# A four-stage graph attention, FFN and Mamba kernel: channel-major first attention, a masked attention that projects last, and a new order of the steps

## The reference, cut to what matters

```
def gat(inp, mask, W, a):
    h = inp @ W
    e = leaky_relu(h @ a[:F] (column) + h @ a[F:] (row), 0.2)
    e = where(mask > 0, e, -9e15)            # not in the first attention
    return elu(softmax(e, axis=2) @ h)

# layer 0
o1  = relu(ln(x) @ mlp1_w + b)               # 256 -> 512
z1  = elu(gat(o1, None, W_fc, a_fc)) + o1    # first attention, 512 channels, no mask
o2  = relu(z1 @ mlp2_w + b)                  # 512 -> 256
x1  = x + relu(elu(gat(o2, adj, W_hand, a_hand)) + o2)    # masked attention "b"
x2  = x1 + ln(x1) + ffn of the 127 nodes with the largest routing weight, times the weight
# layer 1
x3  = x2 + elu(softmax(masked leaky scores) @ (ln(x2) @ W))    # masked attention "g"
out = x3 + mamba2_block(ln(x3))
```

## Time and profile before

| | us |
|---|---|
| median of 3 runs (lowest, highest) | 3889.12 (3888.59, 3889.54) |
| the profiled execution, its own time | 3887.89 |
| its span, first to last instruction | 3886.2 |
| TensorE matmul busy, share of the span | 3668.9, 94% |
| VectorE, ScalarE, GpSimd busy | 3107.9, 2355.4, 1002.1 |
| one full turn (start of L1378 to its next start, from 2008.89) | 57.18 |

### The profile page before, as it was taken

One profiled execution on the slowest core, in us unless ns is written; L12 is line 12 of the kernel. 1 busy time (PEld: TensorE's weight loads), 2 busy tenths in 40 slices (PEclk: granted clock), 3 DMA queues, 4 the chain that ended last, 5 costly groups with the idle time before them and its releaser, 6 DMA issues.

```text
span 3886.2 us, 64302 instructions
## 1 busy us (share of the span) xinstructions
PE 3668.9 (94%) x21016; PEld 3171.3 (82%) x21016; DVE 3107.9 (80%) x8243; ACT 2355.4 (61%) x5250; POOL 1002.1 (26%) x1817
## 2 busy tenths in 40 slices
PE   3789999999999999999999999999999999999985
PEld 2578888888888888888888888888888888888864
DVE  2358888888888888888888888888888888888875
ACT  1246666666666666666666666666666666666654
POOL 0012223223222222322322222232232222223222
PEclk8889999999999999999999999999999999999987
DMA  3000010010011001001001100100100110010000
GB/s 92 11 23 28 30 38 27 30 38 33 24 38 38 27 30 38 27 30 38 32 25 38 38 27 30 38 27 30 38 31 26 38 38 27 30 38 27 30 28 30
DMA packets 73763, 126.85 MB, mean 33 GB/s; under 512 B 9984, under 2 KB 64128, under 8 KB 65536
## 3 DMA queue, kind: packets, MB, share of 16 engines
q1 hardware_dynamic: 73728, 126.42, 9.6%
HBM read 109.10 MB, written 17.30 MB: 33 GB/s over the span
## 4 chain that ended last, share of the span: by engine, by line
PE 68%; DVE 22%; ACT 5%; issue 4%; DVEq 0%; POOL 0%; DMA 0%; POOLq 0%
PE A L1179 12%; PE M L1315 7%; PE A L1199 6%; PE A L1217 6%; PE Q L1303 6%; PE M L1349 6%; PE A L1264 3%; DVE yss L1109 3%; PE A L1226 3%; PE Q L1226 3%; PE Q L1264 3%; DVE u L875 3%; DVE ga_ L1003 2%; PE A L1209 2%; DVE acc L1050 2%
## 5 line engine op out<-in xcount | busy, mean ns | idle before, releaser
L1179 PE MATMUL A<-w_fc,o1T 128*128 128x256 f32 (+1 forms) x2048 | 460.9, 383 | 3.7 <-ACT o1T L619 3.7
L1179 PEld LDWEIGHTS A<-w_fc,o1T 128*128 128x128 f32 x2048 | 382.5, 189 | 65.0 <-ACT o1T L619 5.3
L535 POOL TENSOR_TENSOR var_m<-mv_m,epsilon 128x2 f32<-128x2 f32 x64 | 12.5, 195 | 1414.5 <-DVE mv_m L818 1414.5
L786 ACT ACTIVATE dec<-cumB,cumcol 128x256 f32<-128x256 f32 (+1 forms) x1024 | 366.3, 443 | 0.0
L1041 DVE SCALAR_TENSOR_TENSOR acc<-M,w_conv,acc 128x255 f32<-128x255 f32 (+2 forms) x768 | 315.0, 470 | 0.0
L1315 PE MATMUL M<-xT_m,w_in 128*128 128x256 f32 x1280 | 297.5, 379 | 0.9 <-DVE tz L1083 0.8
L1199 PE MATMUL A<-h,low 128*128 128x257 f32 (+1 forms) x1024 | 256.6, 395 | 22.5 <-DVE low L859 14.0
L1315 PEld LDWEIGHTS M<-xT_m,w_in 128*128 128x128 f32 x1280 | 237.8, 190 | 32.2 <-DVE tz L1083 2.1
L1296 PE MATMUL Q<-selT,w_up 128*128 128x128 f32 x2048 | 249.5, 275 | 0.9 <-ACT selT L722 0.9
L1217 PE MATMUL A<-e,w_mlp 128*128 128x256 f32 x1024 | 242.8, 391 | 1.5 <-DVE e L883 1.5
L1303 PE MATMUL Q<-w_down,gsq 128*128 128x256 f32 x1024 | 237.0, 385 | 7.1 <-DVE gsq L1014 7.1
(11 more groups left out here) (236 smaller groups left out, 8901.8 us busy)
## 6 DMA issues: line engine op xcount, KB each, us to landing
cumB<-cum_dram SPq DMA_DIRECT2D x64, 1024.0 KB, 4.7
x_in<-in_x SPq DMA_DIRECT2D x64, 256.0 KB, 2.8
x<-in_x SPq DMA_DIRECT2D x64, 256.0 KB, 3.0
out<-x3b SPq DMA_DIRECT2D x64, 256.0 KB, 2.9
w_mlp<-in_L_gnn_mlp_w SPq DMA_DIRECT2D x2, 512.0 KB, 5.6
w_fc<-in_L_gnn_W_fc SPq DMA_DIRECT2D x2, 512.0 KB, 6.3
w_up<-in_L_ffn_w SPq DMA_DIRECT2D x1, 1024.0 KB, 10.1
w_down<-in_L_ffn_w SPq DMA_DIRECT2D x1, 1024.0 KB, 11.3
```

Source lines behind the costliest of these rows:

```text
L786: last = nc.scalar.activation(dec[:, h, :], columns[:, h, :], ACT.Relu, bias=cumcol[:, i, h:h + 1], scale=-1.0)
L1179: last = nc.tensor.matmul(rows1(half, u, 2), o1T[:, k, u * P:(u + 1) * P], w_fc[:, k, half, 0:D + 2 * i], start=(k == 0), stop=(k == KH - 1))
```

## The change

It has five parts.

1. **First attention, channel-major.** Everything between `a_fc` and `a_mlp2` now has channels on the partitions. The row sums are formed before the product: `a_sums` (ScalarE: two exp of the spread row, one of the ends, two scaled copies; VectorE: two multiply-max with accumulate, a reciprocal), `a_spread` (TensorE: two transposes; VectorE: one multiply of the factors), `a_low` (ScalarE: two scaled copies, before part of `a_factors`). `a_att` has h1 stationary and p1 moving, so the eight transposes of `a_uturn` and the column of ones are gone. The elu works in halves of 512 columns. `a_mlp1`, `a_turn` and `a_mlp2` all use bank A1, one after the other.
2. **Second masked attention.** The two score columns come from VectorE (four multiply-accumulates over 256 channels, `g_proj`), P @ xn is formed first (`g_att`, turned) and then projected (`g_proj` on TensorE). The four transposes of `g_turn` are gone; ScalarE copies yT instead of xT_g and no longer writes hp_g.
3. **Routing.** `q_route_col` is gone (ScalarE adds the bias to the column), and the rank is one instruction per tile instead of two.
4. **Mamba.** bT and cT get 128 partitions, the upper 64 zero; `m_sq` is two tensor_tensor additions.
5. **A new order and new lags on every engine.** Head steps have lag 0 where they had 1, b_ steps on TensorE 1 where they had up to 2; VectorE now has lags up to 7, ScalarE up to 6, SP up to 8.

```diff
     "tensor": [
+        ("q_gather", 3), ("g_proj", 4), ("a_att.0", 1), ("a_att.1", 1), ("m_cum_col", 5), ("q_ffn1.0", 3),
+        ("q_ffn1.1", 3), ("a_mlp2", 1), ("a_turn", 0), ("m_cb", 5), ("b_proj", 1), ("a_mlp1.0", 0), ("b_bcast", 1),
+        ("b_res", 1), ("m_xrow", 5), ("q_ffn2", 3), ("a_mlp1.1", 0), ("q_scatter", 3), ("m_y.0", 5), ("b_pturn", 1),
+        ("m_y.1", 5), ("b_att", 1), ("a_fc.0", 0), ("m_out", 5), ("m_turn", 4), ("g_bcast", 3), ("m_ss", 5),
+        ("a_fc.1", 0), ("m_dt", 4), ("m_z", 4), ("a_bcast", 0), ("q_route", 2), ("g_pturn", 3), ("m_xbc_a", 4),
+        ("g_att", 3), ("m_xbc_b", 4), ("a_spread", 0), ("m_da", 4),
     "vector": [
+        ("g_proj", 5), ("m_norm", 6), ("b_elu_c", 3), ("b_x1", 3), ("m_sq", 7), ("a_fc", 2), ("g_mask", 5),
+        ("m_ms", 7), ("q_stats", 3), ("a_stats", 0), ("g_lrelu", 5), ("a_fcol", 2), ("m_dt", 6), ("m_out", 7),
+        ("g_max", 5), ("m_gate", 6), ("a_maxima", 2), ("q_rank", 4), ("a_sums", 2), ("g_pturn", 5), ("a_spread", 2),
+        ("m_scan", 6), ("a_probs", 2), ("m_conv_b.0", 6), ("m_conv_b.1", 6), ("m_conv_b.2", 6), ("m_cum_col", 6),
+        ("g_elu_b", 5), ("a_elu_c", 2), ("q_norm", 3), ("q_gelu_a", 4), ("m_silu", 6), ("q_route", 3),
+        ("q_gelu_b", 4), ("a_norm", 0), ("b_proj", 2), ("m_cb", 6), ("q_ffn2", 4), ("m_mix.0", 6), ("b_mask", 2),
+        ("b_lrelu", 2), ("g_x3", 5), ("m_mix.1", 6), ("q_scatter", 4), ("m_stats", 5), ("b_max", 2), ("q_x2", 4),
+        ("g_stats", 4), ("m_y.0", 6), ("m_y.1", 6), ("g_norm", 4), ("b_pturn", 2),
     "scalar": [
+        ("m_decay.1", 6), ("m_xrow", 6), ("a_mlp1", 1), ("b_exp", 2), ("b_pturn", 2), ("b_att", 2), ("b_elu_b", 2),
+        ("m_gated", 6), ("m_turn", 5), ("m_dt_exp", 5), ("g_exp", 4), ("m_z", 5), ("q_route", 3), ("a_fcol", 1),
+        ("g_pturn", 4), ("a_sums", 1), ("m_xbc_a", 5), ("g_turn", 4), ("a_factors", 1), ("m_xbc_b", 5), ("a_low", 1),
+        ("q_gather", 3), ("g_att", 4), ("g_elu", 4), ("a_att", 1), ("a_elu_b", 1), ("m_silu", 5), ("m_decay.0", 5),
+        ("a_mlp2", 1), ("q_gelu_a", 3), ("a_turn", 0), ("q_gelu_c", 3), ("b_proj", 1),
     "gpsimd": [
+        ("m_da", 6), ("a_norm", 0), ("q_norm", 3), ("m_turn", 6), ("m_xrow", 6), ("m_norm", 5), ("q_turn", 3),
+        ("g_norm", 4), ("m_rms", 6), ("m_dt_log", 5),
     "sync": [
+        ("m_spread", 7), ("a_load", 0), ("m_store", 8), ("a_residual", 3),
...
+            def a_sums(b):                                   # ScalarE
+                act.wait_ge(S["gcol_ready"], b)
+                for i, rate in enumerate((1.0, ALPHA)):
+                    last = nc.scalar.activation(brow[:, i, :], A1[:, N:2 * N], ACT.Exp, bias=falls[:, i:i + 1], scale=rate)
+                last.then_inc(S["brow_ready"], 1)
+                act.wait_ge(S["ends_ready"], nth(b, 2, 2))
+                nc.scalar.activation(ends[:], ends[:], ACT.Exp).then_inc(S["ends_exp"], 1)
...
+                    last = nc.scalar.activation(low[:, u, :], brow[:, 1, :], ACT.Copy, scale=ends[:, 1, u:u + 1])
+                last.then_inc(S["part_ready"], 1)
...
+            def a_elu_c(b):                                  # VectorE
+                for i, ps in enumerate((A0, A2)):
+                    v.wait_ge(S["e1x_ready"], nth(b, 2, i + 1))
+                    half = e1[:, 2 * i:2 * i + 2, :]
+                    nc.vector.tensor_tensor(half, two(ps), half, ALU.max).then_inc(S["u1_ready"], 1)
+                for i in range(2):
+                    v.wait_ge(S["u1_ready"], nth(b, 2, i + 1))
+                    half = e1[:, 2 * i:2 * i + 2, :]
+                    nc.vector.scalar_tensor_tensor(out=half, in0=half, scalar=-1.0, in1=o1T[:, 2 * i:2 * i + 2, :],
+                                                   op0=ALU.add, op1=ALU.add).then_inc(S["z1_ready"], 1)
...
+            def g_proj(b):                                   # VectorE
+                v.wait_ge(S["g_xn"], b)
+                before(v, S["g_ue"], b)
+                for u in range(U):
+                    for end in range(2):
+                        last = nc.vector.scalar_tensor_tensor(out=(ea, sc)[end]["g"][:, u, :], in0=xn["g"][:, u, :], scalar=1.0,
+                                                              in1=w_ends[:, end, :], op0=ALU.mult, op1=ALU.mult,
+                                                              accum_out=fc["g"][:, u, end:end + 1])
...
             def m_sq(b):
-                nc.vector.tensor_reduce(yss[:], ysq.rearrange("p k n -> p n k"), AX_X, ALU.add)\
-                    .then_inc(S["yss_ready"], 1)
+                nc.vector.tensor_tensor(ysq[:, 0:2, :], ysq[:, 0:2, :], ysq[:, 2:4, :], ALU.add).then_inc(S["sq_half"], 1)
+                v.wait_ge(S["sq_half"], b)
+                nc.vector.tensor_tensor(yss[:], ysq[:, 0, :], ysq[:, 1, :], ALU.add).then_inc(S["yss_ready"], 1)
...
             def a_att(b, half):                              # TensorE
+                for c in range(2):
                     for j in range(U):
+                        last = nc.tensor.matmul((A0, A2)[half][:, c * N:(c + 1) * N], h1[:, j, half, c * P:(c + 1) * P],
+                                                p1[:, j, :], start=(j == 0), stop=(j == U - 1))
...
-            def a_uturn(b):
-                pe.wait_ge(S["u1_ready"], b)
...
             def a_mlp2(b):
-                pe.wait_ge(S["z1_ready"], b)
+                pe.wait_ge(S["z1_ready"], nth(b, 2, 2))
...
-                a_turn=turn_rows("a", A0, "b_sc"), g_turn=turn_rows("g", Q0),
+                a_turn=turn_rows("a", A1, "o2_ready"), 
```

More of the change, by code:

```diff
@@ L17 @@
 NEG = 9.0e15
+LEAST = 2.0 ** -126
 GELU_CUBE = 0.044715
@@ L29 @@
     "tensor": [
[L30 to L34, removed]
@@ L449, in _ @@
                     last.then_inc(PEs, 1)
+                pe.wait_ge(DV, DV_ENDS)
+                for half in range(2):
+                    for t in range(KD):
+                        last = nc.tensor.transpose(Q0[:, half * D + t * P:half * D + (t + 1) * P],
+                                                   w_gat[:, t, D + half:D + half + 1].to_broadcast([P, P]), ident[:])
+                last.then_inc(PEs, 1)
                 pe.wait_ge(DV, DV_TURNED)
@@ L796, in _ @@
             turns(nc.scalar, "scalar", dict(
-                a_turn=evac_T("a", A0), g_turn=evac_T("g", Q0), m_turn=evac_T("m", M0),
-                a_mlp1=a_mlp1, a_fcol=a_fcol, a_factors=a_factors, a_att=a_att, a_elu_b=a_elu_b, a_mlp2=a_mlp2,
-                b_proj=proj("b", (A0, A2)), g_proj=proj("g", (Q0, Q1)),
-                b_exp=softmax("b"), g_exp=softmax("g"), b_pturn=pturn("b", A2), g_pturn=pturn("g", Q1),
-                b_att=elu_exp("b", A2), g_att=elu_exp("g", Q1), b_elu_b=b_elu_b, g_elu=g_elu,
+                a_turn=evac_T("a", A1), g_turn=g_turn, m_turn=evac_T("m", M0),
+                a_mlp1=a_mlp1, a_fcol=a_fcol, a_factors=a_factors, a_sums=a_sums, a_low=a_low, a_att=a_att, a_elu_b=a_elu_b, a_mlp2=a_mlp2,
+                b_proj=proj("b", (A0, A2)),
+                b_exp=softmax("b"), g_exp=softmax("g"), b_pturn=pturn("b", A0), g_pturn=pturn("g", Q1),
+                b_att=elu_exp("b", A0, -1.0), g_att=elu_exp("g", Q1, 0.0), b_elu_b=b_elu_b, g_elu=g_elu,
                 q_route=q_route, q_gather=q_gather, q_gelu_a=q_gelu_a, q_gelu_c=q_gelu_c,
@@ L880, in a_uturn @@
[L880 to L886 removed]
+                v.wait_ge(S["r1_ready"], nth(b, 2, 1))
@@ L1173, in a_fc @@
             def a_fc(b, i):
-                pe.wait_ge(S["o1_ready"], b)
+                if i == 0:
+                    pe.wait_ge(S["o1_ready"], nth(b, 2, 2))
+                else:
+                    before(pe, S["v1_ready"], b)
                 half = 1 - i
@@ L1189, in a_bcast, with a_spread @@
                     for u in range(U):
-                        last = spread_column(A2[:, half * N + u * P:half * N + (u + 1) * P], f1[:, u, half:half + 1])
+                        last = spread_column(A1[:, half * N + u * P:half * N + (u + 1) * P], f1[:, u, half:half + 1])
                 last.then_inc(S["fb_ps"], 1)
+            def a_spread(b):
+                pe.wait_ge(S["r1_ready"], nth(b, 2, 2))
+                pe.wait_ge(S["h1_a"], b)
+                for u in range(U):
+                    last = spread_column(A0[:, u * P:(u + 1) * P], r1[:, u:u + 1])
+                last.then_inc(S["rb_ps"], 1)
             def a_att(b, half):
```

260 lines of the change are left out of this document (132 added, 128 removed).

## The result

The changed kernel takes 3996.62 us (median of 4 runs, 3994.83 to 4001.50) against 3888.91 of the kernel before in the same comparison: ratio 1.0279, interval 1.0261 to 1.0297. It is slower, as forecast, but by 108 us instead of 15, and outside the range of 3825 to 3955. The profiled execution took 3998.37 us, its span is 3996.7.

What follows compares the result with a forecast made beforehand. TensorE was taken as the bound, but waits would bring the turn to 57.7 us (54.25 work + 3.1 waits + 0.35 restarts) against 57.18: 3887.9 + 30 - 15 gives 3903, or 3904 beside the median; range 3825 to 3955.

Steps and rivals of the forecast that it cites:

- everything asked for is there in time: From a_turn through a_mlp1, b_, m_y and a_fc to the end of m_z, no step would wait for its input.
- I price it at nothing: GpSimd's m_turn waits for the store but ends an estimated 2 us before m_xrow has its input; cost nothing.
- other steps as the closest: Between a_turn and m_z, least time to spare: b_pturn 0.2 to 0.3 us, m_xbc_a 0.4, m_ss 1.3.
- The chain from the end of `m_z`: Through ScalarE, VectorE and a_mlp2 to a_turn, 24.3 us, against 21.2 us of TensorE work; TensorE waits 3.1 a turn.
- what is taken off TensorE comes back as waiting: Full turn: TensorE's work falls 1.27 us to 54.25, but waits make the turn 57.7 us against 57.18.
- rivals 1 and 2: 1: TensorE bound, waits unchanged, 3792 us, chance 0.15 (halfway 3855, 0.17). 2: no change, 3880 to 3896, chance 0.18.
- Rival 3: ScalarE's m_decay.0, 1.1 us to spare, ends late ahead of a_mlp2; 0.9 us a turn, 3960 us, chance 0.12.
- the sum: Whole time: 58 turns at 0.5 us give +30, the drain -15, fill even; 3903, or 3904 beside the median.
- the fill: The fill and 1 us more of setup, taken as even, with 15 us either way.
- the drain: Last five intervals, 245.0 us before: emptier turns earlier give -15 us, bounds nothing and about 10 a turn for two turns.
- the gain of 0.18: m_cb on TensorE: 128 instead of 64 partitions takes 0.66 us instead of 0.84 a turn; bounds no gain and 0.18.
- rival 4: The change doesn't do what it says: m_cb's padding gives nothing, +12 us, inside the range; no chance given.

Runs made afterwards that it cites:

- e1: The changed kernel with GpSimd's multiply of xdt covering 1 of 16 head tiles, the rest staying zero, VectorE's list untouched; 3903.07 us.
- e13: The changed kernel with m_cb's two products over the 64 partitions that hold data instead of 128, in the same place; 4021.66 us.
- e9: The changed kernel with steps reordered on TensorE, VectorE and ScalarE, some steps cut in halves, SyncE's load ahead of its store; 3886.95 us, ratio 0.9998.
- e10: The same as e9, but with SyncE's store ahead of the load; 3919.57 us, ratio 1.0082.

## Why the prediction was right or wrong

**What failed.** Two sentences: "From the start of `a_turn` [...] to the end of `m_z` everything asked for is there in time", and of GpSimd's `m_turn`, "I price it at nothing". I had this stretch at 57.7 - 24.3 = 33.4 us and it took 34.96; with xdt cut short (e1) it took 33.42. I had x3b end 2 us ahead of xdt's input; it ended 0.24 ahead of xdt's start. But that was not the error: I asked only whether xdt would be late for `m_y.0` (it was not), never what runs on VectorE at that moment. So the term that the prediction put at nothing is the time that VectorE stands still under GpSimd: 1.7 us inside `g_x3` (under xdt) and 0.2 in `b_lrelu` (under x3b). With some 0.8 of added work, where I had 0.6, these are VectorE's 2.7 more. 1.14 of it shows as TensorE's wait ahead of `q_scatter`, and with the slower steps behind that wait it is 1.54; the prediction had named other steps as the closest. In the earlier trace rows the shape costs 0.68 or 0.69 throughout, since in the old order no such VectorE instruction started under one of GpSimd's long ones.

**What held.** The chain from the end of `m_z` (2048.5) to `a_turn`, measured against forecast: gcol done 2.65 (2.7), ScalarE through `a_sums` 4.55 (4.55), `a_low` done 9.2 (9.4), `a_probs` done 10.1 (10.25), convolution done 16.2 (16.3), `a_mlp2` 19.34 (19.65), `a_turn` 24.07 (24.3). From start to start the waits cost 1.7 ahead of the second half of `q_ffn1` and `a_mlp2` (2.0) and 1.3 ahead of `a_turn` (1.1). Three rows of it, the step behind the convolution on VectorE, and on ScalarE the end of `m_decay.0` and the step that releases `a_turn`:

```profile
2064.71 0.68 DVE L1005 SCALAR_TENSOR_TENSOR ue_g<-ea_g,ue_g 128x512 f32<-128x512 f32 x1
```
```profile
2069.63 1.92 ACT L830 ACTIVATE dec<-dec 128x2048 f32<-128x2048 f32 x1
2071.60 0.84 ACT L695 ACTIVATE o2T<-A,c_mlp 128x256 f32<-128x256 f32 x2
```

So "what is taken off TensorE comes back as waiting" is right, and rivals 1 and 2 (a shorter chain) are out. Rival 3 is out too, but barely. ScalarE's o2T starts at 2071.60, `a_mlp2` ends at 2071.56 and `m_decay.0` at 2071.55, so `m_decay.0` had next to nothing to spare, and not 1.1 us. The prediction's own list (23.1 for its end, 24.2 less 0.84 for the start behind it) gives 0.3; the 1.1 contradicts it. With the lock nearly taken away (e1) the forecast's turn and time are there within 0.2 and 1 us. The time is so near by luck: in e1 the turns cost 20 us where the sum had 30, the fill 6.6 where it had none, and the drain gave 11.7 where it had 15, and the three misses cancel.

**`m_cb`.** 0.44 and 0.22 against 0.53 and 0.31: the gain of 0.18 that I took from the full-height rows. Experiment e13 shows the height as its cause, and rival 4 is out; with what the two neighbours lose, the 64 rows cost 0.39 us a turn in the new order, twice the term. The rule of the Trainium skill, page "TensorE: Matmul & The Clock Gate", section "Why this matters for your kernels", that a small contraction takes as long as a full one, does not agree with this: with 64 rows instead of 128 the product is slower here, 0.54 against 0.44.

**Fill and drain.** The drain gave 4.7 us, not 15, and the fill cost 7.2, taken as even. Both lie inside their bounds. The profiled execution is 95 us above the sum's 3903; fill and drain are 17 of them, and the other 78 are the 58 turns, 108 us where the sum had 30.

**The range.** It took in only cases built on waits for semaphores. A stall inside an instruction was not among them. By the length of xdt, 1.90 to 2.12 us, an estimate of its worst case would have been some 58 x 1.9 = 110 us, if all of it reached TensorE.

What stays open is why the fill is 7.2 us longer; no run was made for it. The first `m_out` starts at 316.2 in e9 and 313.0 in e10, which differ from the kernel after only in the order of the steps and in steps cut in halves, so it is the order and not the setup that made it late; which step, is not shown.
